# A six-sublayer decoder on one core: when raw weights are loaded, and on which engines they are summed and rounded

## The reference

```python
x = _layernorm(x + _L0_attn_ref(x, ...))                      # 16 heads, rope
x = _layernorm(x + _L0_xattn_ref(x, ctx_1024, ctx_1024, ...)) # 8 heads, gated decay in place of softmax
x = _layernorm(x + _L0_ffn_ref(x, w_gate, w_up, w_down))      # ternary weights, 8-bit activations
x = _layernorm(x + _L1_attn_ref(x, ...))                      # 16 heads
x = _layernorm(x + _L1_xattn_ref(x, ctx_1024, ctx_1024, ...)) # 16 heads, keys and values of ctx
x = _layernorm(x + _L1_ffn_ref(x, W1, b1, W2, b2))            # relu
```

```python
def weight_quant(w):
    scale = 1.0 / jnp.clip(jnp.mean(jnp.abs(w)), EPS, None)
    q = jnp.clip(jnp.round(w * scale), -1.0, 1.0) / scale
```

## Time and profile before

| | us |
|---|---|
| median of 3 runs | 1597.3 (1594.58 to 1601.17) |
| the execution that was profiled | 1596.03 |
| its span, first to last instruction | 1594.0 |
| TensorE busy | 1478.0 |
| VectorE busy | 1146.6 |
| ScalarE busy | 985.3 |
| GpSimd busy | 289.3 |

### The profile page before, as it was taken

The page is one execution under the profiler, slowest core; times in us unless marked ns, Lnnn a source line. Parts: engine busy times, 40 slices in busy tenths (PEclk is TensorE's granted clock), DMA queues, the critical chain, the costliest instruction groups (busy, mean ns, idle before and its releaser), DMA issues. The chain is left out here.

```text
span 1594.0 us, 31275 instructions
## 1 busy us (share of the span) xinstructions
PE 1478.0 (93%) x12244; PEld 961.6 (60%) x12266; DVE 1146.6 (72%) x2007; ACT 985.3 (62%) x1749; POOL 289.3 (18%) x277
## 2 busy tenths in 40 slices
PE   6889999999998998999999998999999999999998
PEld 3555656566675664656766565555676656565657
DVE  3987989856468797865656789876655789986642
ACT  1477666765657755585465865765645686666662
POOL 5121110122221110102222111102122221011010
PEclk8999999999999998999999999999999999999999
DMA  7420243433322112343341121334333202143310
GB/s 252 144 74 28 61 123 111 137 95 108 102 72 61 46 62 59 118 123 106 88 119 54 28 60 30 101 114 116 111 96 93 68 15 67 41 131 109 107 38 30
DMA packets 142721, 139.49 MB, mean 88 GB/s; under 512 B 12914, under 2 KB 128370, under 8 KB 142578
## 3 DMA queue, kind: packets, MB, share of 16 engines
q1 hardware_dynamic: 139714, 131.34, 28.8%
q10 hardware_dynamic: 2864, 6.16, 1.2%
HBM read 68.91 MB, written 42.99 MB: 70 GB/s over the span
## 5 line engine op out<-in xcount | busy, mean ns | idle before, releaser
L1198 DVE TENSOR_REDUCE nm<-psum 128x4 f16<-128x1024 f32 x384 | 453.7, 1223 | 114.4 <-PE psum L785 113.3
L1025 ACT ACTIVATE PB<-psum 128x1024 f32<-128x1024 f32 x288 | 287.5, 1023 | 96.6 <-PE psum L804 94.7
L822 PE MATMUL psum<-PB,V 128*32 128x256 f32 x2304 | 204.7, 385 | 8.8 <-ACT PB L1025 5.1
L1357 POOL TENSOR_TENSOR YX<-YX 128x512 f32<-128x512 f32 x48 | 60.9, 1269 | 598.1 <-ACT YX L1034 598.0
L785 PE MATMUL psum<-QK 48*128 48x256 f16 x1536 | 134.3, 274 | 30.7 <-DMA QK<-heads_dram 10.3
L804 PE MATMUL psum<-QK 49*128 49x256 f16 x1536 | 138.1, 274 | 8.7 <-DVE nm L1198 3.7
L1363 POOL TENSOR_TENSOR XO<-XO,row_b 128x512 f32<-128x512 f32 x80 | 102.5, 1287 | 171.8 <-ACT YX L997 171.8
L688 PE MATMUL psum<-cst 128*128 128x256 f32 x360 | 115.8, 426 | 9.0 <-DMA cst<-in_consts 3.2
L785 PEld LDWEIGHTS psum<-QK 48*128 48x128 f16 x1536 | 57.3, 94 | 102.3 <-issue 52.1
L943 PE MATMUL psum<-YX,W 128*128 128x256 f32 x512 | 118.9, 385 | 0.1
L951 PE MATMUL psum<-W,PB 128*128 128x256 f32 x512 | 117.8, 384 | 0.0
(11 more groups left out here) (172 smaller groups left out, 2702.9 us busy)
## 6 DMA issues: line engine op xcount, KB each, us to landing
QK<-heads_dram SPq DMA_DIRECT2D x96, 512.0 KB, 3.9
heads_dram<-U SPq DMA_DIRECT2D x288, 128.0 KB, 2.0
YX<-U SPq DMA_DIRECT2D x192, 128.0 KB, 3.4
XO<-in_x SPq DMA_DIRECT2D x16, 256.0 KB, 4.2
YX<-in_ctx SPq DMA_DIRECT2D x16, 256.0 KB, 3.6
out<-XO SPq DMA_DIRECT2D x16, 256.0 KB, 2.5
W<-in_w SPq DMA_DIRECT2D x2, 1024.0 KB, 7.0
heads_dram<-PB ACTq DMA_DIRECT2D x4, 256.0 KB, 8.9
```

The lines of the kernel that those rows point to most:

```text
L822: ins = pe.matmul(b[SLOT * j:SLOT * j + SLOT, at:at + TOK], value(L, t, e, u), src, start=(t == 0), stop=(t == TT - 1))
L1025: act.activation(weights_of(L, unit), b[:, 0:1024], ACT.Exp, scale=HD ** -0.5)\
L1198: dve.tensor_reduce(nm[L][:, :, :, unit].rearrange("p t e -> p e t"), b[:, 0:1024].rearrange("p (e t k) -> p e t k", e=2, t=TT), AX.X, ALU ...
```

## The change

- raws waits for the load of lane 3's context instead of for the first qkv weight.
- In the setup list, sums comes before permute. sums moves from VectorE to ScalarE: three activations with the function Abs and an accumulated output, whose elementwise output goes to lane 3's weights buffer; from the second on each waits for the one before.
- ternary moves from VectorE to GpSimd, with the same three passes a weight.
- All five merged orders, the banks and the fills are new. ScalarE: raws, xT of lane 0, then lanes 0 and 1 up to qk, tables, sums, ctx and v of lane 2, permute, negmax of lane 0. GpSimd: both rope halves of lanes 0 and 1, the first of lane 2, ternary 2, ternary 0, the second rope half of lane 2, xb of lane 2, rope of lane 3 with xb of lane 0, ternary 1, heads of lane 0. TensorE: the transposes of lanes 1, 3 and 2 follow lane 0's first rope half; qk of lane 1 comes before rope of lane 2; the product of the sums stands before lane 0's first max; qk.0 of lane 2 stands after lane 1's max.5, with max.6 and lane 0's exp.0 behind it. SyncE: weights 3 stands before lane 1's second stack of the second attention, weights 4 after the load of lane 0's second x. The fills' digits add up to 186, where they were 180; in both, 69 belong to the first batches, and 24 of these to max.

```diff
-    "first": "sp", "raws": "act", "tables": "act", "weights": "sp", "masks": "dve", "permute": "act", "sums": "pe dve", "scales": "dve", "ternary": "dve",
+    "first": "sp", "raws": "act", "tables": "act", "weights": "sp", "masks": "dve", "permute": "act", "sums": "pe act", "scales": "dve", "ternary": "pool",
...
-        steps = [("first", 0), ("raws", 0), ("tables", 0), ("permute", 0), ("sums", 0), ("scales", 0), ("ternary", 2), ("ternary", 0), ("ternary", 1),
+        steps = [("first", 0), ("raws", 0), ("tables", 0), ("sums", 0), ("permute", 0), ("scales", 0), ("ternary", 2), ("ternary", 0), ("ternary", 1),
...
     "act": (
-        "4401200001111322433000220100000300011011311111110120122022022102200010010122220110301120110203103332"
+        "4001200031111442240332002000010033000111011111111012012202022122200001011200222011001211031020310320"
...
     "pool": (
-        "0011002323302111020113021302223301302121303120203001012111220223332003133010211102221003332331132000"
+        "0011244022231303401131001021223320033100112232030031010113112212223220031320003310211223103033323121"
...
                 if name == "raws":
-                    act.wait_ge(qkv_loaded, 16)
+                    act.wait_ge(c_loaded[LANES - 1], 16)
...
+                elif name == "sums":
+                    act.wait_ge(raw_loaded, 48)
+                    for w in range(3):
+                        if w:
+                            act.wait_ge(scaled_w, w)
+                        act.activation(flat(3, 0, 8 * TOK), raw[w], ACT.Abs, accum_out=w_scale[:, w, 0:1]).then_inc(scaled_w, 1)
...
-                elif name == "sums":
-                    dve.wait_ge(raw_loaded, 48)
-                    for w in range(3):
-                        dve.tensor_reduce(w_scale[:, w, 0:1], raw[w], AX.X, ALU.add, apply_absolute_value=True).then_inc(scaled_w, 1)
...
-                elif name == "ternary":
-                    w = unit
-                    dve.wait_ge(scaled_w, SCALED.index("inverse") + 1)
...
             for step in engine_program("pool"):
                 it, name, L, occ, unit = step
-                if name == "rope":
+                if name == "ternary":
+                    w = unit
+                    pool.wait_ge(scaled_w, SCALED.index("inverse") + 1)
+                    if w < 2:
+                        pool.wait_ge(ternary, TERNARY.index("bounded2") + 1)
+                    pool.tensor_scalar(raw[w], raw[w], w_scale[:, w, 2:3], MAGIC, ALU.mult, ALU.add).then_inc(ternary, 1)
+                    pool.wait_ge(ternary, TERNARY.index(f"scaled{w}") + 1)
+                    pool.tensor_scalar(raw[w], raw[w], MAGIC, 1.0, ALU.subtract, ALU.min).then_inc(ternary, 1)
+                    pool.wait_ge(ternary, TERNARY.index(f"whole{w}") + 1)
+                    pool.tensor_scalar(weights_q[w], raw[w], -1.0, None, ALU.max).then_inc(ternary, 1)
+                elif name == "rope":
```

More of the change, by code:

```diff
@@ L212 @@
+        "0112231230322313031220001130312033122132332"),
     "sp": (
[L213 to L216, removed]
+        "0213400100011114304222212330331224330000011141002122200012333310111223010422233013120000313022311111"
@@ new lines @@
+    "0751346520631623064036571642640635164261261037534207501350154275307306416036026305340224624062573505"
+    "3153520634310741045206452027603153703160531075252042460625306420476530723061452072510205702460420247"
+    "0250356130643013613560326530731046242641570743641070254027602645065126032537054205230642370426056025"
+    "6720476420675317042604261420624602025074526040260352037702574041605360241703510451372460124606413615"
+    "6420640724026050324076473140402462035246026470740241064325702406240206370602410357132003126013503206"
@@ new lines @@
+    "0000000001000000000000000000000000000000000000000000000000000000000000000000000000000000000000000000"
+    "0000000000000000000000000000010000000100001000000000000100001100000000000000000000001001000000000000"
+    "0000000001030000000000000100100000010202102010000000000000000000000000000000000000000000000000010000"
+    "0000000000100100000001000002010101000100000000000000010001000000010001000000000000000000000000000000"
+    "00000000000000200100000000100002000000000000000000000000000000000"
@@ L1158, in _ @@
                     dve.tensor_tensor(w_k[:, 1:2], w_k[:, 0:1], w_scale[:, 1, 1:2], ALU.mult).then_inc(scaled_w, 1)
-                elif name == "ternary":
-                    w = unit
-                    dve.wait_ge(scaled_w, SCALED.index("inverse") + 1)
-                    if w < 2:
-                        dve.wait_ge(ternary, TERNARY.index("bounded2") + 1)
-                    dve.tensor_scalar(raw[w], raw[w], w_scale[:, w, 2:3], MAGIC, ALU.mult, ALU.add).then_inc(ternary, 1)
-                    dve.wait_ge(ternary, TERNARY.index(f"scaled{w}") + 1)
-                    dve.tensor_scalar(raw[w], raw[w], MAGIC, 1.0, ALU.subtract, ALU.min).then_inc(ternary, 1)
-                    dve.wait_ge(ternary, TERNARY.index(f"whole{w}") + 1)
-                    dve.tensor_scalar(weights_q[w], raw[w], -1.0, None, ALU.max).then_inc(ternary, 1)
                 elif name == "rope":
@@ L1342, in _ @@
                 setup(pool.memset(GN[L][:, :], 0.0))
+            weights_q = (W_gu[:, 0].rearrange("p k n -> p (k n)"), W_gu[:, 1].rearrange("p k n -> p (k n)"),
+                         W_dn[:, :, :].rearrange("p k n -> p (k n)"))
             own, wait_own = own_work(pool, pool_own)
```

142 lines of the change are left out of this document (66 added, 76 removed).

## The result

The changed kernel takes 1613.2 us (median of 4 runs, 1612.1 to 1616.2), the kernel before, beside it, 1596.7 (1594.6 to 1601.2): ratio 1.0101, 95% interval 1.0082 to 1.0121. The profiled execution has a span of 1610.7 us against 1594.0, 16.7 more. I had forecast 1597, in a range up to 1608. One execution of experiment 2 took 1730 us at a granted clock of 0.84 and is left out of its median.

The account below looks back on a forecast made before the run. TensorE's own work was taken as the bound, busy 1478.0 of 1594.0 us. 1596.0 - 1.4 (first exponential) + 1.4 (GpSimd) - 1.5 (VectorE's relief) + 1.0 (SyncE) + 1.3 (fills) = 1596.8, so 1597 us, range 1585 to 1608.

Parts of the forecast that it names:

- GpSimd holds lane 2's rope: Slower rival: at 5.1 us a rounding pass TensorE stands 15.6 us at lane 2's qk.0, 1611 us; chance 14%.
- Part 4, the price of a pass: Rounding on GpSimd: d, the time of one pass, taken as 2.7 us; lane 2's qk.0 waits, +1.4 us (0 to 15.6).
- half the reads: Argument against slow GpSimd passes: a rounding pass reads one input where the 2.5 ns an element passes read two.
- Part 4, the shared port: VectorE and GpSimd slowing each other: around 50 to 66 us VectorE mostly reads PSUM, so priced at 0.
- hidden in 15 us: Weight 1's three GpSimd passes ahead of lane 0's heads product: 8 us fit in 15 us of GpSimd idle time.
- Part 1, the start: Raw loads wait for the last context, taken at 14.4 us: first rope product at 18.0, -2.6 us (-5.3 to +5.6).
- Part 2, tables and sums: ScalarE's sums end at 48.1; TensorE waits some 3.5 us at their product; first score product at 49.7, +1.4 us.
- Part 3, VectorE's relief: Sums and rounding leave VectorE: first exponential -1.4 us instead of +1.4; a further -1.5 us credited, bounds 0 and -7.5.
- Part 5, SyncE: Late weights (W_1, W_2) cost 0; loads ahead of lane 1's second stack cost +1.0 us (0 to 9).
- Part 6, merges: New orders and banks priced at 0, 6 us either way; six more fill pairs +1.3 us.
- my 4% rival: Faster rival: the new merges find 10 us of TensorE's 80 us of idle time after 200 us, 1587 us; chance 4%.
- a pass of over 4 us: Sign of being wrong: a GpSimd rounding pass takes over 4 us, where 2.7 us was forecast.

Follow-up runs that it names:

- experiment 2: Changed kernel with the raw weights' loads waiting for the first qkv weight again, as before: 1608.4 us, ratio 1.008.
- experiment 1: Changed kernel with the nine rounding passes back on VectorE: 1597.8 us, ratio 1.0011.
- experiment 5: Changed kernel with the second and third rounding pass on GpSimd rewritten in cheap two-operation forms (multiply and add; min and max): 1589.2 us, ratio 0.9955.
- experiment 6: Changed kernel with VectorE's casts of masks moved behind lane 2's last maximum: 1604.6 us, ratio 1.0038.
- experiment 3: Kernel before with only the nine rounding passes moved to GpSimd: 1616.3 us, ratio 1.011.
- experiment 8: Kernel before with only the rounding moved to GpSimd, in the cheap forms: 1595.2 us, ratio 0.9988.
- 7: Kernel before with ScalarE's slot and raw loads put behind the x copies of lanes 0 and 1: 1592.7 us, ratio 0.998.
- experiment 9: Experiment 5 with slot loads behind lane 2's x copy and raw loads behind lane 0's last high halves: 1589.8 us, ratio 0.9951.
- experiment 10: Experiment 5 with the three sums back on VectorE, ahead of lane 1's low halves: 1593.9 us, ratio 0.9992.
- 12: Experiment 5 with SyncE's weights 3 and 4 both back behind lane 1's second stack, as before the change: 1580.9 us, ratio 0.9896.

## Why the prediction was wrong

The time lay outside the range. What happened is the rival that GpSimd holds lane 2's rope, to which I gave 14% and 1611 us.

- **Part 4, the price of a pass: the step that failed.** I took one price, d = 2.7, between 2.0 and 5.1 us. There are three: 2.0, 7.1 and 5.4, on average 4.8; with the gaps between them the six took 29.4 and not 16.2, and the wait was 13.9 and not 1.4. At d = 4.8 my own sum, reach 66.3 and ready 51.5 + 6d, gives 14, and 1609 for the whole. The mechanism and the place were right; the two ends were each some 4 us later than I had them (70.7 and 84.4), which cancels. That the rival's 1611 came so near to 1613.2 is luck in part: its sum holds neither the port (8.6) nor weights 4, nor what the new orders won back. The bounds from the nearest rows didn't hold single passes (7.1 is above the two-input pass), and "half the reads" as the argument against was wrong: what counted was the form. Estimates from the Trainium skill, "GPSIMD Engine Reference", section "3.1 Elementwise — side-by-side cycle accounting", were 3.1 and 1.8 us a pass: the second fits the cheap forms (1.9), neither the others. The advice of that page of the Trainium skill, to leave elementwise work to VectorE, would have been right for these forms (experiment 1) and wrong for the cheap ones (experiment 5).
- **Part 4, the shared port, priced at 0.** I looked for VectorE's work beside the first six passes only. The three casts beside weight 1's passes took 9.6 us instead of 0.9; experiment 6 prices that at 8.6 us, the lag at 8. The rule that I had quoted from the Trainium skill ("SBUF — State Buffer", "Who interferes with whom": each excludes the other for a whole instruction) is what the trace shows: the first cast ended 0.1 us after the 7.1 us pass. With such an instruction on the other side it is dear. Weight 1's passes "hidden in 15 us" was true of GpSimd's own queue and false of its neighbour.
- **Part 1, the start.** Forecast 18.0, measured 21.6 (19.8 to 22.2 in the eight traces with this start, against 20.6 to 22.2 in three with the start of before). ScalarE's and SyncE's timelines:

```profile
4.41 6.72 ACTq L961 DMA_DIRECT2D heads_dram<-PB  x4
19.34 0.43 ACTq L961 DMA_DIRECT2D W_gu<-in_w_down  x1
19.80 0.60 ACTq L961 DMA_DIRECT2D W<-in_w_gate  x1
20.43 0.49 ACTq L961 DMA_DIRECT2D W<-in_w_up  x1
20.97 0.60 ACT L1003 ACTIVATE YX<-psum 128x512 f32<-128x512 f32 x1 [18.96 <-issue]
```

```profile
3.71 10.21 SPq L597 DMA_DIRECT2D YX<-in_ctx  x4
```

  The issues were cheap, as I took them (1.6 us against 3.0), but the last context came at 19.3 and not at 14.4. I had thought that the raw loads held up the contexts. They don't: the last context lands at 17.4 to 19.8 us in the eight traces in which raws waits, at 16.7 to 21.0 in the four in which it doesn't (before, 2, 3, 8), and at 13.0 and 13.3 in the two in which the four slot loads stand later (7 and 9). Those slot loads, 1 MB that ScalarE issues from 4.41 on, are what delays it. That the contexts' issue took 10.2 us here and 2.1 before says nothing of the change: it takes 3.5 to 10.5 us in the traces with this start, 2.1 to 10.4 in the others. The DMA engines in the changed kernel, and in experiment 9 while only slot loads run:

```profile
12.00:14.00 2.00, 0.00 (x0) 0.00 (x0) 0.00 (x0) 0.00 (x0) 0.00 (x0) 0.50 1.03 199
14.00:16.00 2.00, 0.00 (x0) 0.00 (x0) 0.00 (x0) 0.00 (x0) 0.00 (x0) 0.50 0.98 203
```

```profile
20.00:22.00 2.00, 2.00 (x7) 1.00 (x6) 1.47 (x3) 0.00 (x0) 0.53 (x1) 1.00 0.93 98
```

  The 16 DMA engines are fully busy and move 200 GB/s with no raw load among them; slot loads alone keep them 93% busy with 98 GB/s. The bounds, 15.3 to 26.2, held the value; the gain of 2.6 us that I credited didn't come.
- **Part 2, tables and sums.** The sums took 6.1 us, as forecast (three passes of 1.91 us, each with 0.19 for reading the accumulator, partly overlapping). The first score product came at 53.6 against 49.7, and 3.6 of the 3.9 us are Part 1's. The 3.5 us wait at the product of the sums didn't come: I had TensorE there at 44.5, and it came at 52.0, after ScalarE's last sum (51.5). So the forecast of the first score product came near, Part 1 apart, because TensorE was later and not because it waited. Against the sums on VectorE in the new orders (experiment 10) the move is worth 4.8 us, which I had not counted as a gain.
- **Part 3, VectorE's relief, 1.5 us.** Right in the old orders (1 to 2, experiment 8). In the new ones the kernel with cheap passes on GpSimd is 8.6 us faster than with the same work on VectorE (experiments 5 and 1), somewhat over the far bound of 7.5; how much of that is the place at which experiment 1 puts the passes is open.
- **Part 5, SyncE.** The wrong way round. Weights 3, priced at 1.0, cost nothing; weights 4, priced at 0 by its deadline, cost 6.4 us at one wait, because of what was issued right behind it. I had asked who wants W_1 and W_2, and not who stands behind 2 MB on the same engines.
- **Part 6, merges, 0 with 6 either way.** From about 850 us on, every kernel with the new orders gains 7 to 14 us on before (the changed one and experiment 1 11 us each, experiment 1 from +12.7 to +1.7); of those with the old ones experiment 3 loses 1 and experiments 7 and 8 gain 2 and 3. So the new orders, banks and fills win some 10 us late, which was my 4% rival. Which of them, and which of the shuffled steps, does it was not tried.
- What I had named first as making me wrong, a pass of over 4 us, is what happened. Two slips of the sums changed nothing: with passes of 1.8 us they give 1595 and not 1596, and TensorE's idle time after 200 us was 87 us and not 80.

Sum of what was measured: 1613.2 less 1589.2, 24.0, for the forms, and in that the port's 8.6; 8.3 for SyncE's places, by experiments 5 and 12; some 4 for raws; against these stand some 20 that sums, relief and orders would have to have won to leave 16.5. These are differences of single edits, and they needn't add.

## What to carry to other kernels

Before work is moved to an engine that has no row for it, measure the very instruction, operations and operands as written, alone behind the end of the kernel; then count for every long instruction that comes what its neighbour at a shared port does in that time. A transfer has to be priced by what is issued right behind it too, and not by its own deadline alone. When TensorE begins to wait early in a kernel, follow the lag over the whole trace: it shows which losses stay and which parts of a change win something that one total hides.

## What the runs showed that I had not expected

- GpSimd's price for 128x2048 float32 depends on the form by a factor of 3.7 (1.9, 5.4, 7.1 us), and one operation costs more than multiply+add or min+max. Why isn't settled.
- A VectorE cast of 128x128 took 3.80 us beside such a pass, and 0.22 away from it.
- Slot loads of 256 KB alone kept the 16 DMA engines 93% busy with 98 GB/s, and with the contexts beside them fully busy with 200; in before, from 14 to 16 us, raw loads among them took this to 331.
- A start that is 12 us earlier brings 0 to 4 us at the end (experiments 9 and 7): the next thing that is late takes its place.
